# Attention in a fused kernel on one Trainium2 core: query, key and value buffers ordered by group and part, values in rows of 1088 bytes, two groups' loads moved into the scores stage

## The chip, the core and the metric

The kernel runs on one core of a Trainium2 chip. The core has TensorE (PE in the profile, with PEld for its weight loads), VectorE (DVE), ScalarE (ACT), GpSimd (POOL) and SyncE (SP), which here only issues DMA transfers. SBUF and PSUM are the memories on the chip, DRAM is outside. The metric is the device time of one execution in microseconds; lower is better.

## The reference

A chain of four layers on x of 4 x 1024 x 256 (float32): a memory layer, a mixture of experts, an attention layer and the same mixture of experts again. Each takes a layer norm of x and adds its result to x. The change lies in the attention layer:

```python
qkv = x @ Wqkv.T + bqkv
qkv = qkv.reshape(b, n, H, -1).transpose(0, 2, 1, 3)      # H = 16 heads
q, k, v = jnp.split(qkv, 3, axis=-1)                      # 16 elements a head
scores = jnp.einsum('bhqd,bhkd->bhqk', q, k) / scale
attn = jax.nn.softmax(scores, axis=-1)
out = jnp.einsum('bhqk,bhkd->bhqd', attn, v)
out = out.transpose(0, 2, 1, 3).reshape(b, n, -1)
return out @ Wo.T + bo
```

## The kernel before

x stays in SBUF as X, 32 tiles of 128 tokens. The program runs the memory layer, the experts, the attention and the experts again, one after the other. The attention has three stages with a barrier of all engines between them; each engine runs its own list of instructions in order, and semaphores join them.

**The projections** (`qkv_phase`) go through 8 chunks of 512 tokens, numbered 0 to 7; two chunks are one of the 4 batches. For each chunk DVE normalises four tiles (L1484, one chunk ahead), PE transposes them (L1524), ACT copies them out (L1440), PE makes four products of queries and keys (L1544, m = 0 to 3; 0 and 1 are queries) and four of values (L1558). So that bfloat16 products keep float32's accuracy, each query and key is stored as a sum of three bfloat16 parts, high, middle and low: ACT takes the high part (L1445) from PSUM, DVE the remainder (L1506), ACT the middle part (L1450), POOL the low part (L1424). PE has two PSUM banks for these products, so product m waits for the remainder of m - 2. DVE adds the bias to the values (L1511), with a column of ones beside each head. POOL adds the output bias bo to X (L1429).

The parts and values go by SP's DMA to DRAM (`qk_d`, L1391; `v_d`, L1395), and from there back into SBUF in another layout (`load_one`): the 16 heads form 4 groups of 4, and for each group `qs` and `ks` hold six blocks of 16 partitions, one for each pair of parts that is multiplied (`Q_PARTS`, `K_PARTS`), 96 rows, and `va` holds the values. Three more rows follow, -1 in `ks` (POOL's memsets, L1416) and the row maxima of the scores in `qs`, so that one product gives scores minus maximum. `load_group` issues twelve transfers of queries and keys and one of values; SP does this for groups 0 to 3 of batch 0 behind the stores of chunks 1 to 4, after it has waited, in chunk 1, until all stores of chunks 0 and 1 have landed.

From chunk 3 on the row maxima of group 0 are found beside the projections: a unit is one row tile of a head; PE makes its products (L1273 into `psS`) and DVE reduces them (L1288). A unit stands behind every one of the eight products of a chunk; it waits for DVE's reduction of the unit before, and the first for `a.loaded[0]`:

```python
def maxima(c, i):
    for g, v in early_maxima(c, i):
        if v == 0:
            pe.wait_ge(a.loaded[g], 16 * 2 * len(Q_PARTS))
        if (g, v) != (0, 0):
            pe.wait_ge(a.unit_used, g * UNITS + v)
        maximum_products(nc, a, psS, g, v).then_inc(a.unit_done, 1)
```

**The scores** (`scores_phase`) go over 4 batches x 4 groups; a group has 16 slots (two halves of the queries by 8 key tiles). In a slot PE makes the scores of 4 heads, ACT their exponentials (L1663), PE the sums with the values (L1765), and two units of maxima for the next group are made by PE and DVE. At slot 12 PE waits for the loads of the group after the next. POOL splits the maxima into parts (L1296 to L1302), PE transposes them at slots 12 and 13, ACT copies them (L1319), and SP's `place_rows` sends them into `qs` with four transfers (L1326) before the next group begins. SP reloads a group's buffers for the next batch during the group that follows it, one transfer a slot. **The output projection** follows.

Of the kernel before, what the change touches and what calls it, by code (L numbers as in the profile page):

```python
# [12 lines left out]
P = 128  # L13
# [3 lines left out]
KD = D // P  # L17
# [1181 lines left out]
NCH = TOKENS // CW  # L1199
QT = S // P  # L1200
HALF = 512
Q_PARTS = [0, 0, 0, 1, 1, 2]
K_PARTS = [0, 1, 2, 0, 1, 0]
KROWS = len(Q_PARTS) * HD
MROWS = KROWS + 3
VC = HD + 1

# [4 lines left out]
LEAD = 4  # L1212
E_BANKS = 3
PV_COLS = HALF // 2


class HandedOn:
# [29 lines left out]
    return b * (NG * n) + g * n  # L1247


LOADS = 2 * len(Q_PARTS) + 1  # L1250


def load_one(sp, a, b, g, n, qk_d, v_d):

    if n == LOADS - 1:
        sp.dma_start(a.va[g][:, :, :], v_d[b, g, :, :, :]).then_inc(a.v_loaded[g], 16)
        return
    w, i = divmod(n, len(Q_PARTS))
# [70 lines left out]
def attention_phase(nc, tag, X, stats, ident, identb, wqk, wv, bqk, bv, bo, weights_loaded, qk_d, v_d, O):  # L1329

    ctx = ExitStack()
    sems = []
    ctx.callback(release, nc, sems)
    with ctx:
        sb = lambda n, s, d=F32: ctx.enter_context(nc.sbuf_tensor(f"{tag}_{n}", s, d))
        sem = lambda n: new_semaphore(nc, sems, f"{tag}_{n}")
        a = HandedOn(sb, sem)
        qkv_phase(nc, f"{tag}_qkv", X, stats, ident, identb, wqk, wv, bqk, bv, bo, weights_loaded, a, qk_d, v_d)
        scores_phase(nc, f"{tag}_scores", ident, identb, a, qk_d, v_d, O)


def qkv_phase(nc, tag, X, stats, ident, identb, wqk, wv, bqk, bv, bo, weights_loaded, a, qk_d, v_d):

# [6 lines left out]
    with ctx:  # L1350
# [33 lines left out]
        @block.sync  # L1384
        def _(sp):
            for c in range(NCH):
                u = c % 2
                b, half = divmod(c, NCH // B)
                for m in range(NM):
                    sp.wait_ge(lo_ready, c * NM + m + 1)  # L1390
                    sp.dma_start(qk_d[m // KD, :, b, (m % KD) * P:(m % KD + 1) * P, half * CW:(half + 1) * CW]  # L1391
                                 .rearrange("s p t -> p s t"), parts[u][m][:, :, :]).then_inc(parts_stored[u], 16)
                for j in range(CT):
                    sp.wait_ge(v_ready, c * CT + j + 1)
                    sp.dma_start(v_d[b, :, :, half * CT + j, :].rearrange("g p c -> p g c"),  # L1395
                                 vt[u][j][:, :, :].rearrange("p (g h) c -> p g (h c)", g=NG)).then_inc(v_stored[u], 16)
                    if c == NCH - 1 and j == 0:
                        place_rows(sp, a, 0, 0)
                if c == 1:

                    for v in range(2):
                        sp.wait_ge(parts_stored[v], 16 * NM)
                        sp.wait_ge(v_stored[v], 16 * CT)
                if 1 <= c < 1 + NG:
                    load_group(sp, a, 0, c - 1, qk_d, v_d)
            for u in range(2):
                sp.wait_ge(parts_stored[u], 16 * NM * (NCH // 2))
                sp.wait_ge(v_stored[u], 16 * CT * (NCH // 2))

        @block.gpsimd  # L1410
        def _(pool):
            nc.gpsimd.memset(a.zeros[:, :], 0.0).then_inc(a.rows_ready, 1)
            pool.wait_ge(a.rows_ready, 1)

            for g in range(NG):
                nc.gpsimd.memset(a.ks[g][KROWS:MROWS, :, :], -1.0).then_inc(a.rows_ready, 1)  # L1416
                pool.wait_ge(a.rows_ready, g + 2)
            pool.wait_ge(*weights_loaded)
            for c in range(NCH):
                if c == NCH - 1:  # L1420
                    maximum_parts(nc, pool, a, 0, (a.unit_used, UNITS))
                for m in range(NM):
                    pool.wait_ge(mid_ready, c * NM + m + 1)
                    nc.gpsimd.tensor_tensor(parts[c % 2][m][:, 2, :], rest[m][:, :], parts[c % 2][m][:, 1, :],  # L1424
                                            ALU.subtract).then_inc(lo_ready, 1)
                for j in range(CT):

                    pool.wait_ge(n_ready, c * CT + j + 1)
                    nc.gpsimd.tensor_tensor(X[:, c * CT + j, :], X[:, c * CT + j, :], bo[:, :], ALU.add)  # L1429

        @block.scalar
        def _(act):
            nc.scalar.preload_act_table(ACT.Sqrt)
            act.wait_ge(var_done, 1)
            nc.scalar.activation(rstd[:, :], mv[:, :, 1], ACT.Sqrt, bias=eps[:, :]).then_inc(std_done, 1)

            def rows_out(c):
                act.wait_ge(T_done, c + 1)
                for k in range(KD):
                    last = nc.scalar.copy(xT[c % 2][:, k, :], psT[k][:, :])  # L1440
                last.then_inc(xT_ready, 1)

            def high(c, m):
                act.wait_ge(qk_done, c * NM + m + 1)
# [24 lines left out]
        def _(dve):  # L1469
# [24 lines left out]
            for c in range(NCH):  # L1494
# [6 lines left out]
                for m in range(NM):  # L1501

                    dve.wait_ge(hi_ready, c * NM + m + 1)
                    if c:
                        dve.wait_ge(lo_ready, c * NM + m + 1 - NM)
                    nc.vector.scalar_tensor_tensor(rest[m][:, :], psQ[m % 2][:, :], bqk[:, m:m + 1],  # L1506
                                                   parts[u][m][:, 0, :], ALU.add, ALU.subtract).then_inc(rest_ready, 1)
                    maxima(c, m)
                for j in range(CT):
                    dve.wait_ge(v_done, c * CT + j + 1)  # L1510
# [1 line left out]
                                            psV[j % 2][:, 0:D].rearrange("p (h d) -> p h d", d=HD),  # L1512
                                            bv[:, :].rearrange("p (h d) -> p h d", d=HD), ALU.add).then_inc(v_ready, 1)
                    maxima(c, NM + j)

        @block.tensor
        def _(pe):
# [77 lines left out]
    return uses  # L1595


def scores_phase(nc, tag, ident, identb, a, qk_d, v_d, O):

# [9 lines left out]
    with ctx:  # L1609
# [35 lines left out]
        def _(pool):  # L1645
# [87 lines left out]
        def _(pe):  # L1733
# [48 lines left out]
            def slots(b, g, which, first=False, last=False):  # L1782
                nb, ng = following(b, g)
                pb, pg = (b, g - 1) if g else (b - 1, NG - 1)
                for s in which:
# [118 lines left out]
def memory_moe_attention_moe_kernel(nc, x, m0T, w1T, w2T, rates_w, rates_b, gate_w, gate_b,  # L1904
# [3 lines left out]
    with ctx:  # L1908
# [142 lines left out]
```

## Time and profile before

| what | us |
|---|---|
| median of 3 runs (lowest, highest) | 2243.68 (2241.15, 2248.3) |
| profiled execution, its own time | 2245.09 |
| its span | 2243.4 |
| projections, from barrier to barrier | 801.7 to 962 |
| scores | 962 to 1660 |

A row of the timeline gives start, length, engine, line, operation, output and inputs, and the count of merged instructions; in brackets how long the engine was idle before it and who released it. PEclk is the granted clock of PE as a share of 2.4 GHz. SPq is SP's queue, issuing transfers. All times are of one profiled execution.

### The profile page before, as it was taken

Reading aid. Unit: us, or ns where it says so; the run is one execution under the profiler, and the core shown is the slowest. Engines: PE = TensorE matmul, PEld = TensorE weight load, DVE = VectorE, ACT = ScalarE, POOL = GpSimd, SP = SyncE. Lnnn points to the kernel's source line nnn. Section 1 sums busy time; section 2 is a strip of 40 time slices with the busy share of each in tenths; the row PEclk is TensorE's granted clock in tenths of the full one; section 3 lists DMA queues with packets and bytes.
Section 4 is the critical chain, followed back from the end, with each engine's and each line's share of the span. In section 5 each row is a group of like instructions: output and inputs, shape, how many; then the busy total and the mean of one; then the engine's idle time right before and its main releaser. Section 6 shows DMA issues by size and latency. Waiting matters only on the chain. (4 is left out here: it accounts for less than half of the span.)

```text
span 2243.4 us, 51733 instructions
## 1 busy us (share of the span) xinstructions
PE 2090.2 (93%) x18596; PEld 1403.1 (63%) x18597; DVE 1318.9 (59%) x2444; ACT 1020.1 (45%) x2049; POOL 449.9 (20%) x643
## 2 busy tenths in 40 slices
PE   6899799999999958999999999999988999999997
PEld 6577676766666734345556555555548676666665
DVE  5455448222222866789999999999725662222237
ACT  2211122222222123378989898898974222222221
POOL 1022100444444044400000000000000014444420
PEclk9999769999999979999999999999997899999999
DMA  7000010111111329601111111110032001111125
GB/s 282 0 1 0 22 54 3 54 56 56 57 58 54 122 70 218 160 22 45 46 49 40 47 46 46 43 45 20 3 151 93 11 19 57 56 57 58 58 80 178
DMA packets 92766, 142.37 MB, mean 63 GB/s; under 512 B 28724, under 2 KB 65844, under 8 KB 91380
## 3 DMA queue, kind: packets, MB, share of 16 engines
q1 hardware_dynamic: 77620, 98.02, 14.5%
q0 software_dynamic: 14976, 41.96, 5.7%
q8 instruction: 122, 2.00, 0.4%
q14 instruction: 48, 0.39, 0.1%
HBM read 91.04 MB, written 48.50 MB: 62 GB/s over the span
## 5 line engine op out<-in xcount | busy, mean ns | idle before, releaser
L1663 ACT ACTIVATE att_scores_pt<-att_scores_psE 128x512 f32<-128x512 f32 x1024 | 598.4, 598 | 68.4 <-PE att_scores_psE L1273 26.6
L1288 DVE TENSOR_REDUCE att_mx<-att_scores_psS 128x1 f32<-128x1024 f32 x472 | 578.1, 1225 | 50.0 <-PE att_scores_psS L1273 18.9
L592 PE MATMUL moe_ps<-W_gate_up,work 128*128 (+1 forms) x1664 | 535.3, 465 | 2.4 <-ACT work L269 1.2
L1273 PE MATMUL att_scores_psE<-att_qs,att_ks 99*32 99x512 bf16 x4096 | 436.7, 382 | 5.1 <-DVE att_scores_psO L1693 4.3
L592 PEld LDWEIGHTS moe_ps<-W_gate_up,work 128*128 128x128 f32 x1664 | 302.2, 192 | 143.5 <-issue 10.0
L615 PE MATMUL moe_ps<-W_down,moe_hidT 128*128 (+1 forms) x1248 | 318.6, 391 | 15.5 <-DVE moe_hidT L459 4.2
L1765 PE MATMUL att_scores_psO<-att_scores_pt,att_va 128*17 128x256 f32 x4096 | 330.0, 379 | 2.9 <-ACT att_scores_osb L1668 1.3
L1273 PE MATMUL att_scores_psS<-att_ks,att_qs 96*32 96x512 bf16 x3776 | 308.1, 380 | 0.1
L454 DVE TENSOR_TENSOR moe_hid<-moe_silu,moe_ps 128x352 f32<-128x352 f32 x208 | 108.3, 521 | 312.0 <-PE moe_ps L592 312.0
L615 PEld LDWEIGHTS moe_ps<-W_down,moe_hidT 128*128 128x128 f32 x1248 | 221.5, 190 | 65.3 <-issue 36.0
L273 ACT ACTIVATE moe_silu<-moe_ps 128x352 f32<-128x352 f32 x208 | 96.6, 464 | 337.9 <-PE moe_ps L592 337.9
L459 DVE COPY moe_hidT<-moe_ps 128x384 f32<-128x384 f32 x208 | 115.4, 555 | 229.0 <-PE moe_ps L602 229.0
L212 POOL DMA_INDIRECT work<-normalised_rows,moe_now_i x144 | 143.1, 994 | 304.4 <-issue 299.5
L1273 PEld LDWEIGHTS att_scores_psE<-att_qs,att_ks 99*32 99x32 bf16 x4096 | 135.6, 95 | 105.6 <-ACT att_scores_pt L1663 8.5
L1765 PEld LDWEIGHTS att_scores_psO<-att_scores_pt,att_va 128*17 128x17 f32 x4096 | 131.1, 98 | 103.6 <-issue 13.2
L1273 PEld LDWEIGHTS att_scores_psS<-att_ks,att_qs 96*32 96x32 bf16 x3776 | 125.6, 97 | 78.5 <-issue 1.4
L269 ACT COPY work<-moe_ps 128x256 f32<-128x256 f32 x208 | 77.5, 373 | 207.0 <-PE moe_ps L530 207.0
L221 POOL DMA_INDIRECT expert_rows<-work,moe_now_i x144 | 142.8, 992 | 63.1 <-issue 41.9
L530 PE MATMUL moe_ps<-ident,work 128*128 128x128 f32 x544 | 123.2, 314 | 24.2 <-DVE work L322 18.4
L530 PEld LDWEIGHTS moe_ps<-ident,work 128*128 128x128 f32 x544 | 87.5, 177 | 82.8 <-issue 39.2
L1296 POOL TENSOR_TENSOR att_mx<-att_mx,att_zeros 128x32 bf16<-128x32 f32 x16 | 4.2, 261 | 641.5 <-DVE att_mx L1288 641.5
L280 ACT COPY work<-moe_ps 128x256 f32<-128x256 f32 x144 | 53.6, 372 | 173.7 <-PE moe_ps L615 173.7
(266 smaller groups left out, 2030.2 us busy)
## 6 DMA issues: line engine op xcount, KB each, us to landing
work<-expert_rows SPq DMA_DIRECT2D x64, 256.0 KB, 2.8
W_gate_up<-in_gate_up_dram SPq DMA_DIRECT2D x2, 6336.0 KB, 22.0
query_key_parts<-att_qkv_parts SPq DMA_DIRECT2D x32, 384.0 KB, 3.9
att_qs<-query_key_parts SPq DMA_DIRECT2D x96, 128.0 KB, 2.7
att_ks<-query_key_parts SPq DMA_DIRECT2D x96, 128.0 KB, 2.6
normalised_rows<-work SPq DMA_DIRECT2D x64, 128.0 KB, 1.7
W_down<-in_down_a_dram SPq DMA_DIRECT2D x2, 2304.0 KB, 27.0
values<-att_qkv_vt SPq DMA_DIRECT2D x32, 136.0 KB, 4.0
```

Of the source, the lines that this page charges most:

```text
L212: nc.gpsimd.indirect_dma_start(out=src[u][:, :], out_offset=None, in_=xn_d, in_offset=bass.IndirectOffsetOnAxis(ap=now_i[u][:, 0:1].bitcas ...
L221: nc.gpsimd.indirect_dma_start(out=ys, out_offset=bass.IndirectOffsetOnAxis(ap=now_i[u][:, 1:2].bitcast(U32), axis=0), in_=yb[u % 2][:, :] ...
L273: nc.scalar.activation(silu[u][:, :], psG[u][:, 0:I], ACT.Silu).then_inc(silu_done, 1)
L454: nc.vector.tensor_tensor(hid[u][:, 0:I], silu[u][:, :], psU[u][:, 0:I], ALU.mult).then_inc(hid_ready, 1)
L459: nc.vector.tensor_copy(hidT[u][:, :, :].rearrange("p k t -> p (k t)"), psH[:, 0:IP]).then_inc(hidT_ready, 1)
L530: last = nc.tensor.transpose(bank[:, k * P:(k + 1) * P], src[u][:, k * P:(k + 1) * P], ident[:, :])
L592: last = nc.tensor.matmul(bank[u][:, 0:I], srcT[u][:, k, :], W["gate_up"][:, k, e, half * I:(half + 1) * I], start=(k == 0), stop=(k == KD ...
L615: last = nc.tensor.matmul(psD[:, 0:D], hidT[u][:, k, :], W["down"][:, k, e, :], start=(k == 0), stop=(k == KI - 1))
L1273: last = nc.tensor.matmul(out[j:j + 32, :], stationary[:, j:j + 32], moving, start=True, stop=True, tile_position=(0, j), skip_group_check ...
L1288: return nc.vector.tensor_reduce(a.mx[g % 2][:, v:v + 1], bank[:, :, :].rearrange("p h k -> p (h k)"), AX.X, ALU.max)
L1663: nc.scalar.activation(pt[s % 2][:, r, :], psE[use % E_BANKS][:, :], ACT.Exp, scale=HD ** -0.5).then_inc(p_ready, 1)
L1765: last = nc.tensor.matmul(psO[32 * r:32 * r + VC, cols], va[g][:, kt, r * VC:(r + 1) * VC], pt[s % 2][:, r, cols], start=(kt == 0 and part ...
```

## The change

The parts are stored in DRAM by batch, group, part, element, head and token, so that one transfer can load several blocks of 16 partitions: three, two and one, for queries and for keys, six for twelve. For this the weights' columns are ordered by group on the host, keys hold their three parts in reverse order (`part_at`), and each store is split in two, one for each group in the 128 rows. The values are stored for all groups side by side, so that a store writes rows of 1088 bytes and no longer four pieces of 272; a load now reads pieces of 272 bytes where it read rows of 2176. Group 0 is loaded behind chunk 1 as before, group 1 behind chunk 4, and groups 2 and 3 of batch 0 in the first 14 slots of the scores stage. The four memsets of -1 move from POOL at the start of the projections to DVE, one at the end of each of chunks 0 to 3. The 32 additions of bo to X move from POOL in the projections to POOL in the scores stage, two ahead of each group's maxima.

```diff
-Q_PARTS = [0, 0, 0, 1, 1, 2]
-K_PARTS = [0, 1, 2, 0, 1, 0]
-KROWS = len(Q_PARTS) * HD
+PARTS = 3
+PART_RUNS = [(0, PARTS, 0, 0), (3, 2, 0, 1), (5, 1, 0, 2)]
+KROWS = 6 * HD
+def part_at(m, part):
+    return part if m < KD else PARTS - 1 - part
-LOADS = 2 * len(Q_PARTS) + 1
+LOADS = 2 * len(PART_RUNS) + 1
 def load_one(sp, a, b, g, n, qk_d, v_d):
     if n == LOADS - 1:
-        sp.dma_start(a.va[g][:, :, :], v_d[b, g, :, :, :]).then_inc(a.v_loaded[g], 16)
+        sp.dma_start(a.va[g][:, :, :], v_d[b, :, :, g * GROUP * VC:(g + 1) * GROUP * VC]).then_inc(a.v_loaded[g], 16)
         return
-    w, i = divmod(n, len(Q_PARTS))
-    dst, part = (a.qs[g], Q_PARTS[i]) if w == 0 else (a.ks[g], K_PARTS[i])
-    sp.dma_start(dst[i * HD:(i + 1) * HD, :, :],
-                 qk_d[w, part, b, g * GROUP * HD:(g + 1) * GROUP * HD, :]
-                 .rearrange("(r d) t -> d r t", d=HD)).then_inc(a.loaded[g], 16)
+    w, i = divmod(n, len(PART_RUNS))
+    row, count, q_part, k_part = PART_RUNS[i]
+    part = (q_part, k_part)[w]
+    dst = (a.qs, a.ks)[w][g]
+    sp.dma_start(dst[row * HD:(row + count) * HD, :, :].rearrange("p r t -> p (r t)"),
+                 qk_d[w, b, g, part:part + count, :, :, :].rearrange("s d r t -> (s d) (r t)")).then_inc(a.loaded[g], 16)
...
+        STORES = 16 * NM * P // (HD * GROUP)
...
-                    sp.dma_start(qk_d[m // KD, :, b, (m % KD) * P:(m % KD + 1) * P, half * CW:(half + 1) * CW]
-                                 .rearrange("s p t -> p s t"), parts[u][m][:, :, :]).then_inc(parts_stored[u], 16)
+                    for i in range(P // (HD * GROUP)):
+                        rows = slice(i * HD * GROUP, (i + 1) * HD * GROUP)
+                        sp.dma_start(qk_d[m // KD, b, m % KD * (NG // KD) + i, :, :, :, half * CW:(half + 1) * CW]
+                                     .rearrange("s d r t -> (d r) s t"), parts[u][m][rows, :, :]).then_inc(parts_stored[u], 16)
                 for j in range(CT):
                     sp.wait_ge(v_ready, c * CT + j + 1)
-                    sp.dma_start(v_d[b, :, :, half * CT + j, :].rearrange("g p c -> p g c"),
-                                 vt[u][j][:, :, :].rearrange("p (g h) c -> p g (h c)", g=NG)).then_inc(v_stored[u], 16)
+                    sp.dma_start(v_d[b, :, half * CT + j, :], vt[u][j][:, :, :].rearrange("p h c -> p (h c)")).then_inc(v_stored[u], 16)
...
-                if 1 <= c < 1 + NG:
-                    load_group(sp, a, 0, c - 1, qk_d, v_d)
+                    load_group(sp, a, 0, 0, qk_d, v_d)
+                if c == NCH // 2:
+                    load_group(sp, a, 0, 1, qk_d, v_d)
...
         def _(pool):
-            for g in range(NG):
-                nc.gpsimd.memset(a.ks[g][KROWS:MROWS, :, :], -1.0).then_inc(a.rows_ready, 1)
-                pool.wait_ge(a.rows_ready, g + 2)
-            pool.wait_ge(*weights_loaded)
...
-                for j in range(CT):
-                    pool.wait_ge(n_ready, c * CT + j + 1)
-                    nc.gpsimd.tensor_tensor(X[:, c * CT + j, :], X[:, c * CT + j, :], bo[:, :], ALU.add)
...
         def _(dve):
...
                     maxima(c, NM + j)
+                if c < NG:
+                    nc.vector.memset(a.ks[c][KROWS:MROWS, :, :], -1.0)
...
 def scores_phase(...), SP:
+                    if (b, g) == (0, 0):
+                        for n in range((NG - 2) * LOADS):
+                            if n:
+                                sp.wait_ge(pv_done, 2 * n)
+                            load_one(sp, a, 0, 2 + n // LOADS, n % LOADS, qk_d, v_d)
...
 def scores_phase(...), POOL:
+                    for t in range((b * NG + g) * 2, (b * NG + g) * 2 + 2):
+                        nc.gpsimd.tensor_tensor(X[:, t, :], X[:, t, :], bo[:, :], ALU.add)
...
-        qk_d = nc.dram_tensor("query_key_parts", [2, 3, B, D, S], BF16).ap()
-        v_d = nc.dram_tensor("values", [B, NG, P, QT, GROUP * VC], F32).ap()
+        qk_d = nc.dram_tensor("query_key_parts", [2, B, NG, PARTS, HD, GROUP, S], BF16).ap()
+        v_d = nc.dram_tensor("values", [B, P, QT, HEADS * VC], F32).ap()
```

## Rows read from the trace of the kernel before

**Rows 1.** The first line of every answer.

```profile
core 0 of [0], span 2243.4 us
```

**Rows 2.** Busy time by stage: window, length, busy us (instructions), clock, DMA share, GB/s.

```profile
801.70:962.00 160.30, 128.32 (x648) 59.17 (x648) 109.06 (x178) 49.55 (x85) 74.13 (x73) 0.90 0.65 153
962.00:1660.00 698.00, 691.83 (x12216) 391.16 (x12216) 600.11 (x537) 625.75 (x1087) 15.19 (x60) 1.00 0.12 35
```

**Rows 3.** Timeline of the start of the projections, three engines.

```profile
802.01 14.31 POOL L1416 MEMSET att_ks<- 3x4096 bf16 x4 [0.23 <-POOL att_zeros L1412]
...
805.02 11.44 DVE L1484 TENSOR_SCALAR att_qkv_xn<-X,att_qkv_mv,att_qkv_rstd 128x256 f32<-128x256 f32 x4
...
816.52 1.97 PE L1524 MATMUL att_qkv_ps<-ident,att_qkv_xn 128*128 128x128 f32 x8 [22.42 <-DVE att_qkv_xn L1484]
...
818.61 1.38 DVE L1484 TENSOR_SCALAR att_qkv_xn<-X,att_qkv_mv,att_qkv_rstd 128x256 f32<-128x256 f32 x4 [2.14 <-PE att_qkv_ps L1524]
```

**Rows 4.** Timeline of ACT: high parts, m = 0 and 1 of chunk 1, m = 0 after.

```profile
835.64 0.69 ACT L1445 ACTIVATE att_qkv_parts<-att_qkv_ps,Bqk 128x512 bf16<-128x512 f32 x1 [2.95 <-PE att_qkv_ps L1544]
837.35 0.69 ACT L1445 ACTIVATE att_qkv_parts<-att_qkv_ps,Bqk 128x512 bf16<-128x512 f32 x1 [1.03 <-PE att_qkv_ps L1544]
...
858.44 0.69 ACT L1445 ACTIVATE att_qkv_parts<-att_qkv_ps,Bqk 128x512 bf16<-128x512 f32 x1 [3.01 <-PE att_qkv_ps L1544]
...
884.88 0.69 ACT L1445 ACTIVATE att_qkv_parts<-att_qkv_ps,Bqk 128x512 bf16<-128x512 f32 x1 [8.03 <-PE att_qkv_ps L1544]
...
903.74 0.69 ACT L1445 ACTIVATE att_qkv_parts<-att_qkv_ps,Bqk 128x512 bf16<-128x512 f32 x1 [8.02 <-PE att_qkv_ps L1544]
```

**Rows 5.** Timeline of PE in chunk 3.

```profile
863.59 1.05 PE L1273 MATMUL att_qkv_psS<-att_ks,att_qs 96*32 96x512 bf16 x8 [5.24 <-DMA att_ks<-query_key_parts]
```

**Rows 6.** Busy time in two windows of chunk 3.

```profile
860.00:863.00 3.00, 0.00 (x0) 0.00 (x0) 0.00 (x0) 0.00 (x0) 0.00 (x0) 0.92 1.08 147
863.60:869.00 5.40, 5.40 (x20) 1.43 (x20) 1.23 (x1) 0.62 (x2) 0.00 (x0) 0.50 1.14 350
```

**Rows 7.** Timeline of DVE at the program's start.

```profile
1.37 1.98 DVE L1970 MEMSET W_down<- 32x2304 f32 x1 [1.37 <-PEq L2041]
3.42 0.17 DVE L1971 MEMSET ones<- 128x128 f32 x1
```

**Rows 8.** Timeline of DVE at the start of chunks 1 and 4.

```profile
833.92 0.42 DVE L1511 TENSOR_TENSOR att_qkv_vt<-att_qkv_ps,Bv 128x256 f32<-128x256 f32 x1 [0.44 <-PE att_qkv_ps L1558]
...
836.38 0.74 DVE L1506 SCALAR_TENSOR_TENSOR att_qkv_rest<-att_qkv_ps,Bqk,att_qkv_parts 128x512 f32<-128x512 f32 x1
...
884.06 1.38 DVE L1484 TENSOR_SCALAR att_qkv_xn<-X,att_qkv_mv,att_qkv_rstd 128x256 f32<-128x256 f32 x4
...
886.32 1.22 DVE L1288 TENSOR_REDUCE att_mx<-att_qkv_psS 128x1 f32<-128x1024 f32 x1
```

**Rows 9.** Timeline of SP's queue behind chunk 1.

```profile
851.04 2.69 SPq L1260 DMA_DIRECT2D att_qs<-query_key_parts  x6
```

**Rows 10.** Busy time at the end of the projections, the last value stores.

```profile
957.00:960.00 3.00, 1.05 (x11) 0.16 (x9) 2.21 (x3) 0.00 (x0) 0.00 (x0) 1.00 0.62 141
```

**Rows 11.** Timelines of DVE and POOL in chunk 3.

```profile
877.08 1.23 DVE L1288 TENSOR_REDUCE att_mx<-att_qkv_psS 128x1 f32<-128x1024 f32 x1 [0.16 <-PE att_qkv_psS L1273]
...
877.26 2.78 POOL L1429 TENSOR_TENSOR X<-X,Bo 128x256 f32<-128x256 f32 x4
```

**Rows 12.** Busy time around three idle times of PE.

```profile
790.11:794.10 3.99, 1.56 (x7) 1.06 (x6) 3.83 (x10) 0.00 (x0) 0.00 (x0) 1.00 0.38 131
84.99:87.73 2.74, 0.00 (x1) 0.00 (x0) 2.25 (x14) 0.00 (x0) 0.00 (x0) 0.99 0.00 0
87.73:91.00 3.27, 3.27 (x8) 2.54 (x9) 0.00 (x0) 0.00 (x0) 0.00 (x0) 0.50 0.00 0
248.98:252.64 3.66, 0.00 (x0) 0.00 (x0) 1.73 (x10) 0.00 (x0) 1.01 (x1) 0.85 0.00 0
252.64:256.00 3.36, 2.93 (x8) 2.26 (x8) 1.15 (x3) 0.00 (x0) 0.00 (x0) 0.50 0.00 0
```

More of the change, by code:

```diff
@@ L1337, in attention_phase, with qkv_phase @@
         a = HandedOn(sb, sem)
-        qkv_phase(nc, f"{tag}_qkv", X, stats, ident, identb, wqk, wv, bqk, bv, bo, weights_loaded, a, qk_d, v_d)
-        scores_phase(nc, f"{tag}_scores", ident, identb, a, qk_d, v_d, O)
-def qkv_phase(nc, tag, X, stats, ident, identb, wqk, wv, bqk, bv, bo, weights_loaded, a, qk_d, v_d):
+        qkv_phase(nc, f"{tag}_qkv", X, stats, ident, identb, wqk, wv, bqk, bv, weights_loaded, a, qk_d, v_d)
+        scores_phase(nc, f"{tag}_scores", X, ident, identb, bo, a, qk_d, v_d, O)
+def qkv_phase(nc, tag, X, stats, ident, identb, wqk, wv, bqk, bv, weights_loaded, a, qk_d, v_d):
     ctx = ExitStack()
@@ L1401, in _ @@
                     for v in range(2):
-                        sp.wait_ge(parts_stored[v], 16 * NM)
+                        sp.wait_ge(parts_stored[v], STORES)
                         sp.wait_ge(v_stored[v], 16 * CT)
-                if 1 <= c < 1 + NG:
-                    load_group(sp, a, 0, c - 1, qk_d, v_d)
+                    load_group(sp, a, 0, 0, qk_d, v_d)
+                if c == NCH // 2:
+                    load_group(sp, a, 0, 1, qk_d, v_d)
             for u in range(2):
-                sp.wait_ge(parts_stored[u], 16 * NM * (NCH // 2))
+                sp.wait_ge(parts_stored[u], STORES * (NCH // 2))
                 sp.wait_ge(v_stored[u], 16 * CT * (NCH // 2))
@@ L1423, in _ @@
                     pool.wait_ge(mid_ready, c * NM + m + 1)
-                    nc.gpsimd.tensor_tensor(parts[c % 2][m][:, 2, :], rest[m][:, :], parts[c % 2][m][:, 1, :],
+                    nc.gpsimd.tensor_tensor(parts[c % 2][m][:, part_at(m, 2), :], rest[m][:, :], parts[c % 2][m][:, 1, :],
                                             ALU.subtract).then_inc(lo_ready, 1)
-                for j in range(CT):
-                    pool.wait_ge(n_ready, c * CT + j + 1)
-                    nc.gpsimd.tensor_tensor(X[:, c * CT + j, :], X[:, c * CT + j, :], bo[:, :], ALU.add)
         @block.scalar
@@ L1444, in high @@
                 act.wait_ge(qk_done, c * NM + m + 1)
-                nc.scalar.activation(parts[c % 2][m][:, 0, :], psQ[m % 2][:, :], ACT.Identity,
+                nc.scalar.activation(parts[c % 2][m][:, part_at(m, 0), :], psQ[m % 2][:, :], ACT.Identity,
                                      bias=bqk[:, m:m + 1]).then_inc(hi_ready, 1)
@@ L1455, in _ @@
                 if c >= 2:
-                    act.wait_ge(parts_stored[c % 2], c // 2 * 16 * NM)
+                    act.wait_ge(parts_stored[c % 2], c // 2 * STORES)
                 for m in range(NM):
@@ L1506, in _ @@
                     nc.vector.scalar_tensor_tensor(rest[m][:, :], psQ[m % 2][:, :], bqk[:, m:m + 1],
-                                                   parts[u][m][:, 0, :], ALU.add, ALU.subtract).then_inc(rest_ready, 1)
+                                                   parts[u][m][:, part_at(m, 0), :], ALU.add, ALU.subtract).then_inc(rest_ready, 1)
                     maxima(c, m)
@@ L1529, in maxima @@
                     if v == 0:
-                        pe.wait_ge(a.loaded[g], 16 * 2 * len(Q_PARTS))
+                        pe.wait_ge(a.loaded[g], 16 * (LOADS - 1))
                     if (g, v) != (0, 0):
@@ L1595, in exps_of, with scores_phase @@
     return uses
-def scores_phase(nc, tag, ident, identb, a, qk_d, v_d, O):
+def scores_phase(nc, tag, X, ident, identb, bo, a, qk_d, v_d, O):
     ctx = ExitStack()
@@ L1790, in slots @@
                     if s == SLOTS - LEAD and units:
-                        pe.wait_ge(loaded[mg], mb * (16 * 12) + 16 * 12)
+                        pe.wait_ge(loaded[mg], mb * (16 * (LOADS - 1)) + 16 * (LOADS - 1))
                     def earlier_sums(part):
@@ L2022 @@
     bqkv = att("bqkv").reshape(HEADS, 3, HD)
+    by_group = lambda v: v.reshape(NG, GROUP, *v.shape[1:])
     experts = lambda n: np.concatenate([moe("w_" + n), moe("sw_" + n)[None]])
@@ L2035 @@
         "router": tiles(np.concatenate([moe("gate_w"), moe("shared_gate_w")]).T),
-        "wqk": tiles(wqkv[:, 0:2].transpose(3, 1, 0, 2).reshape(D, 2 * D)),
+        "wqk": tiles(by_group(wqkv[:, 0:2]).transpose(4, 2, 0, 3, 1).reshape(D, 2 * D)),
         "wv": tiles(wqkv[:, 2].transpose(2, 0, 1).reshape(D, D)), "wo": tiles(att("Wo").T),
-        "bqk": bqkv[:, 0:2].transpose(1, 0, 2).reshape(2 * KD, P).T,
+        "bqk": by_group(bqkv[:, 0:2]).transpose(2, 0, 3, 1).reshape(2 * KD, P).T,
         "bv": bqkv[:, 2].reshape(1, D), "bo": att("bo").reshape(1, D),
```

## The prediction

> **What bounds the kernel now.** I read the span first [rows 1], and then the busy time by stage: the scores stage has 692 us of PE (TensorE) work in 698, the stage of the projections, at 801.7 to 962, only 128 in 160 [rows 2]. Time can be got or lost in the second. The chain of waits on the timeline shows where.
>
> At its start POOL sets four rows of -1 in 14.31 us; beside it DVE takes 11.44 us for four normalisations, where four of the same form take 1.38 once POOL is done. DVE stands behind POOL, and PE begins at 816.52 after 22.42 us of waiting for DVE [rows 3].
>
> ScalarE's activations start as each product of 512 tokens ends, so they give the pace [rows 4]. Chunk 4 takes 18.86 us (884.88 to 903.74), with eight maxima woven in; chunk 3 takes 26.44 (858.44 to 884.88), 7.58 more. PE there waits 5.24 us for group 0's keys, until 863.59 [rows 5], and by then its granted clock has fallen to 0.5 (1.2 of 2.4 GHz), where it stays until about 869 [rows 6]. So the loss is 5.24 us of waiting and 2.34 of slower work.
>
> **The change, part by part.**
>
> *POOL's four memsets go.* The first four normalisations take 1.38 instead of 11.44 us: -10.06. PE still idles for 12 us before it, so its clock there is low in both kernels; I give that nothing.
>
> *They come back on DVE*, one at the end of each of chunks 0 to 3, 4096 elements a partition each. No DVE memset of bf16 is in the trace. Those of f32 are: 2304 elements in 1.98 us and 128 in 0.17 [rows 7], so (1.98 - 0.17) / 2176 = 0.832 ns an element and 0.06 fixed; 4096 cost 3.47 us. From above: DVE's next instruction starts 2.05 us after the first one [rows 7], so at most 0.89 ns, 3.65 us. From below: half the price per element for bf16, 1.77 us, or a quarter, 0.91. I take 3.47, since POOL's bf16 memsets, the nearest by type, cost 0.87 ns an element (14.31 / 4 / 4096) [rows 3], no less than f32.
>
> What waits behind one: DVE's next normalisations and then the first remainder (L1506) of the next chunk, which frees the bank for PE's third product. In chunk 1 DVE is free at 834.34, normalises until 836.4, and the remainder ends at 837.12 [rows 8]; PE's second product ends as its activation starts, at 837.35 [rows 4], so 0.2 us are to spare. With the memset: 834.34 + 3.47 + 1.38 + 0.75 = 839.94. (The normalisations take 1.38 and not 2.2, since POOL's adds to X are gone from beside them.) PE's third product starts at 839.95 for 837.35: +2.6. Chunk 2 the same: +2.6. In chunk 3 the second unit of maxima waits for the reduction (1.22) behind that remainder: DVE is free 1.3 us before the first activation (858.44), as in chunk 1 (834.34 against 835.64), at 857.1; + 3.47 + 1.38 + 0.75 + 1.22 = 863.9. Without a late load the reduction would end as in chunk 4, 2.66 us after the activation (887.54 - 884.88), at 861.1: +2.8. In chunk 4 the same chain starts after the last reduction, at 884.06 [rows 8]; and PE's second unit waits for its end: 884.06 + 3.47 + 1.38 + 0.75 + 1.22 = 890.9 against 887.54: +3.35. Together 2.6 + 2.6 + 2.8 + 3.35 = +11.35 us.
>
> The Trainium skill, VectorE: DVE Perf Modes (Zero memsets can be issued as uint32), says that a memset takes one cycle per element whatever the type, at 0.96 GHz; an estimate from it is 4096 / 0.96 = 4.27 us. By it the four delays would be 14.55 us and the span 3.2 us longer than by the row, in the case below where the change hardly shows. The trace's 0.83 to 0.89 ns an element lies under its 1.04, and the row decides.
>
> *Chunk 3's wait for the keys goes.* Before, SP issued the twelve loads from 851.04 on [rows 9], after chunk 1's stores had landed, and the keys were there at 863.59 [rows 5], 12.5 us later, with the DMA engines full at 147 GB/s [rows 6]. PE came for them at 863.59 - 5.24 = 858.35. Now chunk 1's value stores have 128 rows of 1088 bytes each for 512 of 272, and should land a little sooner; I count 0 to 2 us, bounded by the 2.0 us of DMA time of such stores below. With the same bytes at the same rate and a start 1 us sooner, the keys are there at 862.6 on the old scale. PE comes at 858.35 + 2.6 (chunk 2's memset delay) = 860.95, and a first unit late by up to 3 us is covered by chunk 3's own memset. So nothing of the 7.58 is left: -7.58. Memsets and load cover one another; were the memsets cheap, part of the wait would come back.
>
> *Stores, order of parts, two loads moved.* 64 stores of queries and keys for 32, at 0.36 us to issue and eight in a chunk of 11 us: SP has room. The order of the six parts alters the addresses of the same instructions: nothing. Group 1's load goes behind chunk 4, its first use is in chunk 7. Groups 2 and 3 load in the first 14 slots of the scores stage, DMA share 0.12 [rows 2], needed at slot 12 and one group later. The values' loads get 1024 pieces of 272 bytes; the projections' last three stores, 1536 such pieces, took 0.62 x 3 = 1.86 us of full DMA [rows 10], so one load about 1.2 us. Only the very last of the 14 matters: it stands in SP's queue just ahead of the four transfers of maxima for group 1 due some two slots later (698 / 16 groups / 16 slots = 2.7 us each [rows 2]). Cost 0, bounds 0 and +1.2, the one load's own time. The same last three stores end the stage; with a quarter of the pieces I give -0.4, bounds 0 and -1.86.
>
> *32 additions to X on POOL* (2.78 us for four [rows 11]) go from the projections to the scores. Beside four of them DVE's reduction takes 1.23 us [rows 11], as everywhere; POOL has 15 us of work in 698 there [rows 2], and two of them stand ahead of a wait of most of a group. Nothing. Uncovered they would cost 32 x 0.7 = 22 us.
>
> *The granted clock.* This is the disputed term. PE now idles for 2.6, 2.6, about 3.2 and 3.65 us in chunks 1 to 4. In the trace 2.43 us of idle time (from 790.11) left the clock at 1.00; 2.74 us (to 87.73) and 3.66 us (to 252.64) were each followed by work at 0.50 [rows 12]. A fall that ends as the one in chunk 3 did costs 2.34 us. Bounds: no fall, 0; four, 9.4. I take half of one, +1.1, as a point between none and one, since the shortest of these gaps are near the one that left the clock alone.
>
> Sum: -10.06 + 11.35 - 7.58 - 0.4 + 1.1 = -5.6 us. The span of 2243.4 [rows 1] becomes 2237.8; the profiled execution's own time 2245.09 becomes 2239.5. It lies 1.4 us above the median of the three runs (2243.68), so the median becomes 2238.1.
>
> **The rivals.**
>
> *Cheap memsets (0.17).* If bf16 costs half (1.77 us), the delays are 0.9, 0.9, 1.2 and 1.65, or 4.65; some 2 us of the keys' wait stays (862.6 against 858.35 + 0.9, less 1.2 under chunk 3's memset): -10.06 + 4.65 - 7.58 + 2.1 - 0.4 = -11.3, 2232.4 us. At a quarter the delays are about 1.2 and the wait 4.2: -12.6, 2231.1. For it: normalisations of 256 elements take 1.38 / 4 = 0.35 us each [rows 3], so DVE passes more than one element in 0.83 ns in some forms. Against: the memset rows, DVE's and POOL's.
>
> *The clock falls in every gap (0.09), the slower side.* Place: the four gaps of PE in chunks 1 to 4. Price 2.34 each: -6.7 + 9.4 = +2.7, 2246.4 us. It decides from three falls on (-6.7 + 7.0 = +0.3). For it: the 2.74 us gap that ended low. Against: the 2.43 us that left the clock alone, and two of the four gaps, 2.6 us, lie between these.
>
> *The loads of few partitions and long rows land late (0.06).* A load is now 16, 32 or 48 partitions with 8 KB each. The point from which it counts is about 864 on the old scale (860.95 + 3); at half the present rate they would land near 850 + 25 = 875, and PE would stand 11 us more: -5.6 + 11 = about +5, 2249 us. For it: the trace has no load of that form, and 147 GB/s is already poor beside the 350 just after [rows 6]. Against: the bytes and partitions are the same, in fewer and longer rows.
>
> *The change hardly shows (0.18).* What the start wins is given back: the memsets cost 3.65 (+0.7), the clock falls once or twice (+2.3 to 4.7), the transfers of maxima +1.2, nothing comes at the end (+0.4): -6.7 + 4.6 to 7.0, so -2 to 0, near 2242.5.
>
> **The numbers.** My forecast, 2238.1 with -8 to -3.5 as its own range (2235.7 to 2240.2), has 0.50. Within 0.3% is ±6.7 us here, about what three runs between 2241.15 and 2248.3 can tell from no change. The sum lies just inside that bound; without a fall it is -6.7, on it. So of its 0.50 I give 0.20 to faster and 0.30 to the same; cheap memsets 0.17 to faster, and the last three (0.33) to the same but for 0.05, late loads worse than priced, and 0.01 faster. Faster 0.38, same 0.57, slower 0.05. Range: from the cheap memsets' 2230.5 to 2246.4, the clock's.
>
> **What would show it.** Right: PE's first transposition at about 806.5 and not 816.5; DVE memsets of 3 x 4096 bf16 at 3.47 us; waits of PE's products for L1506 of about 2.6 us in chunks 1 and 2; no wait of PE for att_ks from the DMA; chunk 3 near 21.7 us and chunk 4 near 22.2; the scores stage at 698 us. Wrong: a memset under 2 us, granted clock at 0.5 inside chunks 1 to 5, PE waiting for loads or for the maxima's rows in the scores stage, or a stage outside attention that changes its length.

## The result, and the profile after

The changed kernel takes 2250.82 us (median of 20 runs, 2246.82 to 2254.76), the kernel before 2245.45 (20 runs, 2241.15 to 2252.01). The ratio is 1.0021, 95% interval 1.0012 to 1.0029: slower by 2.7 to 6.5 us, where 5.6 us less were forecast. The profiled execution has a span of 2247.2 us for 2243.4 [rows 1].

All of it that is not scatter lies in the stage of the projections. Outside the attention the code is the same, and there the profiled executions of all kernels below differ by themselves: the stage begins 801.7 to 806.5 us into the span, and 580 to 586 us follow the scores. So I compare the stage and not the span. I measure the stage from DVE's first memset in it to its memset of psO at the start of the scores: 160.40 us before (801.73 to 962.13), 164.35 after. Busy time by stage of the changed kernel, columns as in [rows 2]:

```profile
803.32:967.67 164.35, 132.56 (x648) 60.48 (x648) 110.14 (x183) 50.09 (x85) 37.92 (x38) 0.92 0.50 127
967.67:1665.30 697.63, 692.04 (x12216) 390.48 (x12216) 599.75 (x536) 625.64 (x1087) 37.05 (x92) 1.00 0.16 40
```

The scores stage is unchanged (697.4 us before by the same marks), with 22 us more POOL work and a DMA share of 0.16 for 0.12 [rows 2]: the additions to X and the loads moved there cost nothing.

The start went as forecast. Timeline of the changed kernel's first rows, which answer to [rows 3]:

```profile
806.62 1.38 DVE L1484 TENSOR_SCALAR att_qkv_xn<-X,att_qkv_mv,att_qkv_rstd 128x256 f32<-128x256 f32 x4
...
808.05 1.97 PE L1526 MATMUL att_qkv_ps<-ident,att_qkv_xn 128*128 128x128 f32 x8 [12.36 <-DVE att_qkv_xn L1484]
```

Four normalisations take 1.38 us for 11.44, and PE's wait is 12.36 us for 22.42: exactly 10.06 less.

Then comes the loss. DVE at the end of chunk 0 and the start of chunk 1:

```profile
825.85 0.42 DVE L1511 TENSOR_TENSOR att_qkv_vt<-att_qkv_ps,Bv 128x256 f32<-128x256 f32 x1 [0.44 <-PE att_qkv_ps L1560]
827.19 3.47 DVE L1516 MEMSET att_ks<- 3x4096 bf16 x1 [0.91 <-issue]
830.68 1.38 DVE L1484 TENSOR_SCALAR att_qkv_xn<-X,att_qkv_mv,att_qkv_rstd 128x256 f32<-128x256 f32 x4
831.97 1.40 DVE L1506 SCALAR_TENSOR_TENSOR att_qkv_rest<-att_qkv_ps,Bqk,att_qkv_parts 128x512 f32<-128x512 f32 x2
```

The memset's row says 3.47 us, to the hundredth what was worked out. But it begins 0.91 us after DVE has finished the values (825.85 + 0.42 = 826.27), and nothing is there to wait for ("issue"). From neighbour to neighbour it holds DVE for 830.68 - 826.27 = 4.4 us, 1.07 ns an element. PE's gaps behind the four memsets:

```profile
832.77 3.70 PE L1546 MATMUL att_qkv_ps<-att_qkv_xT,Wqk 128*128 128x512 f32 x8 [3.52 <-DVE att_qkv_rest L1506]
847.75 5.40 PE L1546 MATMUL att_qkv_ps<-att_qkv_xT,Wqk 128*128 128x512 f32 x8 [3.52 <-DVE att_qkv_rest L1506]
865.57 1.04 PE L1279 MATMUL att_qkv_psS<-att_ks,att_qs 96*32 96x512 bf16 x8 [3.91 <-DVE att_mx L1294]
...
891.59 0.62 PE L1279 MATMUL att_qkv_psS<-att_ks,att_qs 96*32 96x512 bf16 x8 [4.53 <-DVE att_mx L1294]
```

They are 3.52, 3.52, 3.91 and 4.53 us where 2.6, 2.6, about 3.2 and 3.65 were expected. The same eight instructions take 3.70 us after the first gap and 5.40 after the second: the clock has fallen there. Busy time in windows around gaps two, three and four:

```profile
848.20:851.40 3.20, 3.20 (x5) 1.30 (x4) 0.16 (x1) 0.20 (x2) 1.16 (x1) 0.50 1.03 177
861.70:865.50 3.80, 0.00 (x0) 0.00 (x0) 3.79 (x8) 1.30 (x2) 0.39 (x1) 0.95 0.35 124
865.50:871.50 6.00, 5.93 (x21) 1.73 (x22) 2.32 (x4) 1.14 (x2) 0.77 (x1) 0.50 0.26 66
887.10:891.50 4.40, 0.00 (x0) 0.00 (x0) 4.38 (x8) 1.30 (x2) 0.37 (x1) 1.00 0.00 0
891.50:895.50 4.00, 3.91 (x12) 1.09 (x12) 1.92 (x3) 0.00 (x0) 0.79 (x1) 0.61 0.39 98
```

Of four gaps three end with the granted clock at 0.50 (1.2 GHz), in the fourth window for most of it (mean 0.61). The activations at each chunk's start, as in [rows 4], give the sum:

```profile
827.57 0.69 ACT L1445 ACTIVATE att_qkv_parts<-att_qkv_ps,Bqk 128x512 bf16<-128x512 f32 x1 [2.95 <-PE att_qkv_ps L1546]
...
842.62 0.69 ACT L1445 ACTIVATE att_qkv_parts<-att_qkv_ps,Bqk 128x512 bf16<-128x512 f32 x1 [3.01 <-PE att_qkv_ps L1546]
...
859.30 0.69 ACT L1445 ACTIVATE att_qkv_parts<-att_qkv_ps,Bqk 128x512 bf16<-128x512 f32 x1 [3.01 <-PE att_qkv_ps L1546]
...
884.70 0.69 ACT L1445 ACTIVATE att_qkv_parts<-att_qkv_ps,Bqk 128x512 bf16<-128x512 f32 x1 [8.03 <-PE att_qkv_ps L1546]
...
909.38 0.69 ACT L1445 ACTIVATE att_qkv_parts<-att_qkv_ps,Bqk 128x512 bf16<-128x512 f32 x1 [8.03 <-PE att_qkv_ps L1546]
```

Chunks 1 to 4 take 15.05, 16.68, 25.40 and 24.68 us; before, 11.38, 11.42, 26.44 and 18.86. PE's list of waits has no entry for the keys any more.

### The profile page after: what moved, and what is told of

It reads as the page before. It is cut to its first block and busy times, and to the rows that moved or that the text cites. A ratio compares the mean times of both kernels' runs of the same rounds, so it can differ in the third digit from the quotient of the medians.

```text
span 2247.2 us, 51669 instructions
## 1 busy us (share of the span) xinstructions
PE 2096.2 (93%) x18596; PEld 1405.3 (63%) x18597; DVE 1320.6 (59%) x2448; ACT 1020.8 (45%) x2049; POOL 435.4 (19%) x639
```

## Experiments

"Stage" is the stage of the projections by the marks above, from one profiled execution of each kernel, and so are the chunks; whether the clock falls in the same gaps in every execution, no run shows. "First wait" is PE's wait for group 0's keys in chunk 3. The ratio comes from all runs of a kernel.

| run | stage, us | first wait | chunks 1 to 4, us | ratio to the kernel before (95%) |
|---|---|---|---|---|
| before | 160.40 | 5.24 | 11.38, 11.42, 26.44, 18.86 | 1 |
| changed | 164.35 | none | 15.05, 16.68, 25.40, 24.68 | 1.0021 (1.0012 to 1.0029) |
| e1 | 147.34 | 3.27 | 11.37, 11.43, 23.79, 18.87 | 0.9942 (0.9928 to 0.9955) |
| e2 | 157.88 | 3.50 | 11.37, 11.43, 23.66, 18.87 | 0.9987 (0.9978 to 0.9996) |
| e3 | 149.80 | 2.03 | 12.92, 12.85, 20.85, 20.91 | 0.9943 (0.9896 to 0.9989) |
| e4 | 161.71 | 1.53 | 15.05, 16.67, 22.43, 24.70 | 1.0011 (0.9997 to 1.0024) |
| e5 | 158.13 | 0.30 | 15.05, 14.98, 22.42, 24.70 | 0.9979 (0.9970 to 0.9989) |
| e6 | 150.64 | 4.74 | 11.37, 11.43, 25.13, 18.87 | one run |
| e7 | 146.77 | 2.86 | 11.38, 11.43, 22.97, 18.87 | one run |
| e8 | 143.98 | 1.31 | 11.37, 11.43, 20.13, 18.87 | 0.9915 (0.9901 to 0.9928) |
| e9 | 150.96 | 5.76 | 11.38, 11.43, 26.80, 18.86 | 0.9959 (0.9945 to 0.9973) |

The scores stage is 696.7 to 697.8 us in all eleven. Chunk 0 takes 11.3 to 12.5 us, by when the clock rises in it.

**e1: the memsets on POOL, late.** Everything of the change is kept but the place of the memsets.

```diff
 POOL, behind the low parts of chunk c:
+                if c >= NCH - NG:
+                    pool.drain()
+                    nc.gpsimd.memset(a.ks[c - (NCH - NG)][KROWS:MROWS, :, :], -1.0)
+                    pool.drain()
 DVE:
-                if c < NG:
-                    nc.vector.memset(a.ks[c][KROWS:MROWS, :, :], -1.0)
```

> The changed kernel with the four memsets of -1 taken off DVE and given to POOL behind its last low part of chunks 4 to 7. All times here are of the stage of the projections, from DVE's first memset to its memset of psO: 160.40 us in the kernel before, 164.35 in the changed one. Theory A: the memsets on DVE are the whole loss. A memset there holds DVE for 4.4 us (3.47 in its row and 0.91 idle ahead of it), and with three falls of PE's clock the four cost 21.7 us. Without them the stage loses 21.7 us, gets about 3.3 us of the wait for group 0's keys back and perhaps one fall (2.3): 146.0 to 148.4 us, ratio to the kernel before 0.994 to 0.995. POOL's memsets lie in its 8 us of idle time beside reductions and cost nothing. Rival B: the memsets cost what was predicted, 11.35 us, and the rest of the loss comes from the stores in halves or the load of few partitions: 153 us or more. Rival C: POOL's memsets meet DVE's normalisations there too: up to 3.5 us each in chunks 4 to 7, 14 us back.

147.34 us: theory A, and neither rival. The stage is 17.0 us shorter without the DVE memsets. They cost more than that by themselves (21.3 us: 15.1 of delay and 6.2 of slower clock, added up below), but had covered 3.27 us of waiting for the keys and a fall of the clock behind it (23.79 - 18.87 = 4.9 us in chunk 3). Chunks 4 to 7, where POOL's memsets now lie, keep their 18.87 us. The timelines of POOL and DVE in chunk 4 show why:

```profile
883.67 3.51 POOL L1432 MEMSET att_ks<- 3x4096 bf16 x1
...
884.45 0.41 DVE L1515 TENSOR_TENSOR att_qkv_vt<-att_qkv_ps,Bv 128x256 f32<-128x256 f32 x1
885.25 1.23 DVE L1294 TENSOR_REDUCE att_mx<-att_qkv_psS 128x1 f32<-128x1024 f32 x1 [0.39 <-PE att_qkv_psS L1279]
```

Beside the memset DVE has only reductions and additions out of PSUM, and they keep their 1.23 and 0.41 us; it is the normalisations, SBUF to SBUF, that stood behind it at the start [rows 3].

**e2: the memsets back on POOL at the start.** The edit is the removed loop of the change put back, with its waits, and the DVE memsets taken out.

> The changed kernel with the four memsets of -1 back on POOL at the start of the projections, all else as changed. Theory A: the start costs its 10.1 us again, the 21.7 us of the DVE memsets go, and of the wait for the keys about 3.3 us (5.6 with a fall of the clock) is back: stage of the projections 156.0 to 158.4 us (160.40 before, 164.35 changed), ratio 0.998 to 0.999. Rival B, the new stores, loads and moved additions cost time by themselves: 163 us or more, ratio above 1.001.

157.88 us and 0.9987: as theory A has it. All of the change but the memsets is a small gain; rival B falls. So does the prediction's rival of loads that land late: where PE waits for them, the keys of the six new loads are there 10.7 to 11.2 us after SP's first issue (e1, e2, e3, e5, e6 and e8), those of the twelve old ones 12.5 to 13.5 us after it (before, e4, e9). e2's chunk 3 is 2.78 us shorter than before and nothing else in the stage differs by more than chunk 0's scatter.

**e3: the same bytes in half the elements.**

```diff
-                    nc.vector.memset(a.ks[c][KROWS:MROWS, :, :], -1.0)
+                    nc.vector.memset(a.ks[c][KROWS:MROWS, :, :].rearrange("p r t -> p (r t)").bitcast(F32), -1.0058...)
```

The constant is the float32 whose bytes are twice those of -1 in bfloat16.

> The changed kernel with each DVE memset written through a float32 view, two values of -1 an element, so 2048 elements for 4096 with the same bytes. Theory A (1.07 ns an element in truth, 4.4 us for 4096): 2.2 us less a memset, delays of 1.3, 1.3, 1.5 and 2.1, gaps of PE under 2.5 us, no fall of the clock in chunks 1, 2 and 4, about 1 to 1.5 us of the keys' wait back: stage about 150 to 151.5 us. By the row alone (0.832 ns) each is 1.7 us shorter: about 2 us longer than that. If the memset's cost is not by the element (a fixed wait of 0.91 us ahead of it stays): the row shows 1.77 us and the idle time ahead of it is still 0.91. By theory A that idle time halves too, to about 0.45.

Timeline of DVE in chunk 0 to 1:

```profile
828.26 0.42 DVE L1511 TENSOR_TENSOR att_qkv_vt<-att_qkv_ps,Bv 128x256 f32<-128x256 f32 x1 [0.44 <-PE att_qkv_ps L1560]
829.16 1.76 DVE L1516 MEMSET att_ks<- 3x2048 f32 x1 [0.48 <-issue]
830.94 1.38 DVE L1484 TENSOR_SCALAR att_qkv_xn<-X,att_qkv_mv,att_qkv_rstd 128x256 f32<-128x256 f32 x4
```

The idle time ahead of the row halves with the row, 0.48 for 0.91, so it belongs to the memset: 830.94 - 828.68 = 2.26 us for 2048 elements, 1.10 ns each. From the two lengths together, (4.41 - 2.26) / 2048 = 1.05 ns an element and 0.1 us fixed, so the cost goes by the element and not by a fixed wait. The type makes no difference that shows. Chunk 1 is 2.13 us shorter than in the changed kernel, the difference of the two memsets (4.4 - 2.26). The gaps behind DVE are 1.39, 1.39 and 2.40 us in chunks 1, 2 and 4, the wait for the keys in chunk 3 is 2.03 us, and the clock stays up in all of them. 149.80 us is just under the forecast's lower end; the interval of the ratio is too wide to tell e3 from e1.

**e4: this one part in the kernel before.** The kernel before, with the four memsets on DVE as in the changed one.

> The kernel before with one edit: the four memsets of -1 go from POOL at the start to DVE at the end of chunks 0 to 3, as in the changed kernel. Twelve loads, old layouts, additions to X in the projections. Theory A: this one part carries the whole result: -10.1 at the start, delays of about 15 us and two to four falls, the keys' wait hidden; normalisations beside POOL's additions take 0.8 us more in each of three chunks: stage 164 to 168 us. Rival B: 150 to 155, since the loss would be in the stores and loads.

161.71 us: 6.7 above rival B's range and 2.3 under theory A's. Chunks 1, 2 and 4 are those of the changed kernel to 0.02 us. Chunk 3 is 22.43 for 25.40: here the keys came 1.53 us late, PE's one gap of 3.91 us was two (1.53 and 2.31 us), and the clock did not fall. So the chunk with a second wait is 3 us shorter; that the split did it is argued from this one profile, no run changes it alone. The profiled execution was also the fastest of its ten (2243.48 us, median 2250.05). The ratio, 1.0011, does not tell the kernel from the one before.

**e5: PE kept at work in the gaps.** Three products whose result is not used, where PE would wait:

```diff
                     last.then_inc(qk_done, 1)
+                    if m == 1 and 1 <= c <= NG:
+                        pe.wait_ge(v_ready, c * CT)
+                        for x in range(3):
+                            nc.tensor.matmul(psV[0][:, :], wqk[:, 0, 0:P], xT[u][:, 0, :], start=True, stop=True)
                     maxima(c, m)
```

> The changed kernel, memsets on DVE as they are, with three products of 512 tokens (2.7 us, into a free bank, their result is not used) given to PE behind the second product of chunks 1 to 4, where it waits for DVE. DVE's chain is as long as before. Theory A (the rows of e4 bear on it): the delays by DVE are 15.1 us (3.67, 3.67, 3.55, 4.2) and stay; the three falls of the granted clock cost 1.6, 3.0 and 1.6 us, 6.2 together, and go: stage of the projections 158.2 us for 164.35, chunks 1 to 4 at 15.05, 15.05, 22.4, 23.1. Rival: the clock is a symptom, PE waits for DVE anyway, and the stage stays at 164 us; or the added products are themselves in the way and it grows.

Timeline of PE in chunk 2 (L1552 are the added products), and the window behind the fourth gap:

```profile
842.18 2.74 PE L1552 MATMUL att_qkv_ps<-att_qkv_xT,Wqk 128*128 128x512 f32 x6
845.86 3.70 PE L1546 MATMUL att_qkv_ps<-att_qkv_xT,Wqk 128*128 128x512 f32 x8 [0.94 <-DVE att_qkv_rest L1506]
```

```profile
885.40:888.80 3.40, 3.40 (x12) 1.18 (x4) 1.46 (x2) 0.00 (x0) 0.33 (x1) 0.50 0.46 116
```

With 11 us (4 times 2.7) more work for PE the kernel is faster than the changed one: 0.9979 to the kernel before for 1.0021. PE's next product comes when it did (chunk 1: 15.05 both times), but chunk 2 is 14.98 for 16.68 and chunk 3 22.42 for 25.40. Those are the prices of two falls, 1.7 and 3.0 us. That the total of 158.13 met my 158.2 was in part luck: the clock still fell in chunk 4 (24.70 us for the 23.1 expected), after a gap of 1.96 us, and the stretch ahead of chunk 1 was 1.5 us shorter (22.73 for 24.25) because the clock rose earlier in chunk 0.

**e6, e7: other parts of the change undone in e1.** e6 has the old layout of the values in DRAM (store and load as before), e7 the additions to X on POOL in the projections.

> e1 (memsets on POOL in chunks 4 to 7) with the old layout of the values in DRAM: stores of 512 pieces of 272 bytes, loads of 128 rows. If the new layout of the values brings the keys earlier, PE's wait for them in chunk 3 grows from 3.27 us by up to 1.5; if the transfer of queries and keys in fewer and longer rows does it, the wait stays at 3.3. The end of the stage: up to 0.4 us later. Stage 147.3 to 149.2 us.

> e1 with the 32 additions to X on POOL in the projections, as in the kernel before, and not in the scores stage. Expected: stage 147.3 us within 0.5 and scores stage 697 us as before: the additions cost nothing in either place (normalisations of 2.2 us for 1.38 in chunks 0 to 2 have 0.2 us of cover). Rival: they cost up to 0.8 us in each of three chunks, 149.7 us.

e6: 150.64 us, 3.3 more, and 1.4 above the forecast's upper end. 1.34 are in chunk 3, where the keys come 1.47 us later: SP issues their first load 6.20 us ahead of the chunk for 8.03 in e1, since it waits for the value stores. 0.7 is chunk 0's scatter. 1.25 is at the end of the stage, where DVE idles 3.67 us for 2.42 before its memset of psO. I had given 0.4 for that. The stage ends when the last stores have landed, and SP's queue and the landing can be read apart: from the start of chunk 7 to the end of SP's last issue, and from there to the memset.

| kernels | query and key stores | values' pieces, bytes | last issue, us after chunk 7's start | memset of psO, us later |
|---|---|---|---|---|
| before, e4, e9 | whole | 272 | 16.89 to 16.90 | 3.76, 3.98, 4.25 |
| e6 | in halves | 272 | 18.06 | 3.75 |
| changed, e1, e2, e3, e5, e7, e8 | in halves | 1088 | 17.87 to 17.92 | 2.63 to 2.65 |

The stores in halves keep SP 1.0 us longer, and the longer rows land 1.1 us or more sooner; in the changed kernel the two cancel. So the new layout of the values is worth about 2.6 us (1.34 + 1.25), by e6 alone. The rival that only the transfer of queries and keys brings the keys earlier falls.

e7: 146.77 us, 0.6 less than e1. Chunk 3 is 0.82 us shorter, half of it in the wait for the keys (2.86 for 3.27) and half in the clock behind it, and chunk 0 is 0.25 longer. Chunks 1 and 2 are the same to 0.01 us and the scores to 0.5. The additions cost nothing that shows in either place.

**e9: the late memsets alone, in the kernel before.** e1's edit in the kernel before, behind the additions.

> The kernel before with one edit: POOL's four memsets of -1 go from the start of the projections to behind its additions in chunks 4 to 7. Twelve loads, old layouts, additions in the projections. Expected by theory A: the start gives its 10.1 us and chunk 3's wait for the keys stays at 5.2 us and one fall of the clock: stage 150.3 us for 160.40, ratio 0.9955. The difference to e1 (147.34 us) is then what the new layouts, loads and stores give in all, 3 us, almost all of it in chunk 3. Rival: with POOL's additions ahead of them the memsets reach into DVE's normalisations of chunks 4 to 7 and give part of it back.

150.96 us, 0.9959: the memsets moved by themselves are about seven tenths of what e1 gives (9.4 of 13.1 us). The rest of the change adds 3.6 us (147.34). The rival falls: chunks 4 to 7 keep their 18.86 to 18.87 us. PE's wait for the keys is 5.76 us for 5.24 before with the same loads, which shows the size of the scatter.

**e8: loads issued earlier.** e1, and SP does not wait for chunk 1's value stores before it loads queries and keys:

```diff
                     for v in range(2):
                         sp.wait_ge(parts_stored[v], STORES)
-                        sp.wait_ge(v_stored[v], 16 * CT)
-                    load_group(sp, a, 0, 0, qk_d, v_d)
+                    for n in range(LOADS - 1):
+                        load_one(sp, a, 0, 0, n, qk_d, v_d)
+                if c == 2:
+                    for v in range(2):
+                        sp.wait_ge(v_stored[v], 16 * CT + 16 * CT * (v == 0))
+                    load_one(sp, a, 0, 0, LOADS - 1, qk_d, v_d)
```

> e1 with group 0's six loads of queries and keys issued when the query and key stores of chunks 0 and 1 have landed, without waiting for the value stores; the values' load goes behind chunk 2. In e1 the loads wait for the last value store. Expected: loads start about 1.9 us sooner, PE's wait for the keys falls from 3.27 to about 1.4 us, the clock does not fall in chunk 3 (1.7 us more): stage 143.5 to 144.5 us, ratio to the kernel before 0.992 to 0.9935. Rival: the transfer is bound by something else than its start (the stores of chunk 2 that go with it) and the wait stays near 3 us.

PE's first unit of maxima in e1 and in e8:

```profile
851.62 0.61 PE L1279 MATMUL att_qkv_psS<-att_ks,att_qs 96*32 96x512 bf16 x8 [3.27 <-DMA att_ks<-query_key_parts]
852.17 3.68 PE L1548 MATMUL att_qkv_ps<-att_qkv_xT,Wqk 128*128 128x512 f32 x4
```

```profile
850.74 0.61 PE L1279 MATMUL att_qkv_psS<-att_ks,att_qs 96*32 96x512 bf16 x8 [1.31 <-DMA att_ks<-query_key_parts]
851.29 1.98 PE L1552 MATMUL att_qkv_ps<-att_qkv_xT,Wqk 128*128 128x512 f32 x4
```

The wait is 1.96 us shorter, and the product behind it takes 1.98 us for 3.68: no fall. SP issued the first load 9.45 us ahead of chunk 3 for 8.03, 1.4 us sooner and not 1.9; where the other 0.5 us comes from is open. The stage is 143.98 us, as forecast, and the ratio 0.9915, just under the forecast's 0.992. At a median of 2229.46 us it is the fastest version; its stage is 20.4 us shorter than the changed kernel's and 16.4 shorter than before's.

## Why the prediction was wrong, step by step

*Start, -10.06.* Right: 22.42 to 12.36 us. Off POOL alone it gives the same in e9 (12.34).

*The keys' wait, -7.58.* Right in the changed kernel, and right that memsets and wait cover one another: without memsets on DVE 3.27 us of waiting came back (e1), with half their elements 2.03 (e3).

*The memsets, +11.35. This step failed.* The mechanism was right, and the term was mis-sized by its price: "4096 cost 3.47 us". The row reads that, but DVE is held for 4.4. The chunks give delays of 3.67 (15.05 - 11.38) in chunks 1 and 2; 3.55 in chunk 3 (22.42 in e5 - 18.87); and 4.2 in chunk 4 (20.91 - 18.87 = 2.04 in e3, and 2.14 for the other half of the memset). Together they are 15.1 us, so the term was 3.7 too small. The bound from above, 3.65 us from the start of the next instruction, looked on the wrong side: the hidden part lies ahead of the row, not behind it. The Trainium skill, VectorE: DVE Perf Modes (Zero memsets can be issued as uint32), gave one cycle an element, with that page's 0.96 GHz an estimate of 4.27 us. The runs agree with it to 0.15 us (4.41), against the row on which I let the case rest. With bf16 no cheaper than float32, the rival of cheap memsets falls too. The trace of before could have told. The first rows of POOL and SP in the program's body, beside DVE's memset of W_down [rows 7]:

```profile
0.82 0.20 POOL L1976 MEMSET ident<- 128x128 f32 x1 [0.29 <-POOLq L2041]
0.83 2.05 SPq L1961 DMA_DIRECT2D X<-in_x_dram  x4
```

POOL and SP go at 0.82, DVE's memset shows only at 1.37. If DVE went with them, which the trace does not show, 2304 elements took 0.55 + 1.98 = 2.53 us, 1.10 ns each, as in e3.

*The clock, +1.1. Failed too, and it is the larger part of the miss.* The half fall was a point between none and one. Three of four gaps ended in a fall: 1.63 us in chunk 2 (16.68 - 15.05), 2.98 in chunk 3 (25.40 - 22.42), 1.6 in chunk 4 (24.68 - 18.87 - 4.2), 6.2 together. The price per fall that I took, 2.34, lies among them; the number of falls was wrong. That was the rival with the falls in every gap, which I had at 0.09. In part the step before caused it: 0.9 us more of memset made gaps of 3.52 out of 2.6, and with gaps of 1.39 to 2.40 us (e3) no fall is left. No run has gaps of 2.6, 3.2 and 3.65 us, so how many falls those would have ended in stays open.

*The end, -0.4.* 2.53 to 2.42 us, -0.1. This term was two: 1.1 us won by the values' longer rows and 1.0 lost by the stores in halves (the table at e6), for which I had written that SP has room. It has none at the end of chunk 7, nor ahead of group 0's loads: with whole stores (before, e9) the first load is issued 7.40 and 7.69 us ahead of chunk 3, with halves and the same pieces of values (e6) 6.20. The parts' order, the additions and the two loads moved cost nothing, as forecast; the scores stage differs by 0.2 us, so the transfers of maxima behind the last load cost nothing either.

With 0.4 us more in chunk 0 the sum is -10.06 + 15.1 + 6.2 - 7.58 - 0.1 + 0.4 = +4.0, and the stage is longer by 3.95. Of the 9.5 us between that and the forecast 3.7 are the memsets' price, 5.1 the clock, 0.3 the end and 0.4 the scatter of chunk 0. The ratio's interval, 2.7 to 6.5 us, holds the 4.0; the medians' +5.4 leaves 1.4 us that no profile traces, inside that interval. The range was too low at its upper end, 2246.4, because its rival of four falls kept the cheap price of the memsets; its lower end, 2230.5, lies 0.6 under the lowest time worked out, 2231.1, and nothing hangs on that.

## What to carry to other kernels

Take an instruction's price from the end of its neighbour before to the start of the one behind, in a stretch where the engine waits for nothing; where no such stretch is shown, the row's own length is a lower bound only. A small fill costs by its elements in a partition: three partitions of 4096 held DVE for 4.4 us here. So it belongs on an engine with idle time and beside work that it does not hold up (here POOL, which idles for 11 us between the low parts of two late chunks, at a time when DVE only reduces and adds out of PSUM), or into half as many elements of twice the width. Where a delay opens gaps in TensorE's work, work out the gap and not only the delay: here three falls of the clock cost 6.2 us on top of 15.1 us of delay.

## What the runs showed of the hardware

A DVE memset takes 1.07 to 1.10 ns an element in both types tried (4.4 us for 4096 of bfloat16, 2.26 for 2048 of float32), and its row shows 0.85 to 0.86 ns of it; the rest (0.91 and 0.48 us) stands ahead of the row as idle time with no releaser.

POOL memsets beside DVE's SBUF to SBUF normalisations held them up until the last one had ended (four in 11.44 us in the kernel before and in e2, 1.38 without it in e1 and e9), and did not touch reductions or additions that read PSUM (e1: 1.23 and 0.41 us).

A gap's length alone does not settle whether PE's clock falls. In chunks 1 to 4 of the eleven kernels gaps of 2.86 us and more ended at 1.2 GHz, but for the first of two gaps of 3.52 us, in the changed kernel and again in e4. Gaps of 2.40 us and less left the clock at 2.4 GHz, but for one of 1.96 us in e5. A fall cost 1.2 to 3.0 us (1.2 in e7, 22.97 - 18.87 - 2.86), and added work in the gaps won two of them back.
